# Where an attention loop issues its fills and weight loads: ahead of a turn's values, or behind them

## The reference

```python
x = x + jnp.tanh(g_xattn[0]) * _L0_xattn_ref(_layernorm(x), ctx_2048, ctx_2048)
x = x + jnp.tanh(g_ffn[0])   * _L0_ffn_ref(_layernorm(x), w_gate, wi_0, wi_1, wo)   # 8 experts, 2 per token
x = x + jnp.tanh(g_xattn[1]) * _L1_xattn_ref(_layernorm(x), ctx_2048, ...)          # scan over the context
x = x + jnp.tanh(g_ffn[1])   * _L1_ffn_ref(_layernorm(x), ...)                      # 64 experts, 4 per token
```

```python
qh = q.reshape(bs * 8, ch, T); kh = k.reshape(bs * 8, ch, S); vh = v.reshape(bs * 8, ch, S)
attn = softmax(einsum('bct,bcs->bts', qh * scale, kh * scale), axis=-1)
out  = einsum('bts,bcs->bct', attn, vh)
```

## Time and profile before

| what | value |
|---|---|
| time, median of 3 runs | 1125.35 us (1125.19 to 1127.35) |
| profiled execution | 1120.38 us, its span 1118.6 us |
| mean granted TensorE clock | 0.966 |
| TensorE busy | 1029.7 us, 92% |
| VectorE, ScalarE, GpSimd busy | 724.5, 500.5, 589.1 us |
| moved by DMA | 199.49 MB, mean 178 GB/s |

### The profile page before, as it was taken

How to read it: one execution, slowest core, us unless ns; L and a number is a source line. 1 busy time by engine, 2 the same in 40 slices (tenths; PEclk the granted TensorE clock), 3 DMA queues, 4 the chain that set the end, 5 groups by cost and what they waited for, 6 DMA issues and landing times. The chain is left out here.

```text
span 1118.6 us, 18847 instructions
## 1 busy us (share of the span) xinstructions
PE 1029.7 (92%) x5364; PEld 740.6 (66%) x5364; DVE 724.5 (65%) x1703; ACT 500.5 (45%) x880; POOL 589.1 (53%) x556
## 2 busy tenths in 40 slices
PE   5799999999878999999799999999999999999960
PEld 3455656655326777777279568578788888888850
DVE  4477777777547888887488438348415666666750
ACT  3375575564327888887342031221313333333320
POOL 6367767666324666667543646356342344434551
PEclk9899999999979999999899999999999999999985
DMA  9965556763543333332540231033269999999729
GB/s 285 348 211 186 165 186 222 246 221 119 198 146 126 124 103 106 105 108 85 186 159 1 107 113 56 25 128 106 89 221 324 337 325 309 287 312 341 194 27 194
DMA packets 128254, 199.49 MB, mean 178 GB/s; under 512 B 35975, under 2 KB 44167, under 8 KB 128186
## 3 DMA queue, kind: packets, MB, share of 16 engines
q1 hardware_dynamic: 106538, 160.66, 42.9%
q0 software_dynamic: 21360, 37.48, 13.3%
q10 hardware_dynamic: 288, 0.52, 0.1%
HBM read 133.10 MB, written 87.56 MB: 197 GB/s over the span
## 5 line engine op out<-in xcount | busy, mean ns | idle before, releaser
L935 POOL TENSOR_TENSOR m_down_lo<-wo,m_down_hi 128x512 fp32r<-128x512 f32 x78 | 129.4, 1679 | 75.9 <-ACT m_down_hi L1030 75.9
L543 PE MATMUL bank<-win,vT 128*128 128x512 f32 x256 | 124.4, 600 | 0.0
L703 DVE TENSOR_REDUCE negmax<-bank 128x1 bf16<-128x512 f32 x128 | 85.8, 674 | 46.0 <-PE bank L550 45.5
L633 ACT ACTIVATE win<-bank 128x512 f32<-128x512 f32 x128 | 69.4, 594 | 89.9 <-PE bank L535 89.4
L1044 DVE TENSOR_TENSOR m_up_lo<-w,m_up_hi 128x1024 fp32r<-128x1024 f32 x78 | 97.7, 1254 | 13.4 <-ACT m_up_hi L1002 11.9
L2035 POOL DMA_INDIRECT out<-m_y,m_token x32 | 50.7, 1586 | 85.3 <-DMA out<-m_y,m_token 34.1
L1264 POOL DMA_INDIRECT tab<-stage_up,slot x64 | 66.0, 1031 | 51.2 <-DVE slot L1610 33.3
L2065 PE MATMUL bank<-y,m_w 128*128 128x128 f32 x736 | 89.7, 275 | 0.0
L2035 POOL DMA_INDIRECT sums<-m_y,m_token x32 | 52.1, 1629 | 70.9 <-DVE m_y L2129 40.0
L2065 PEld LDWEIGHTS bank<-y,m_w 128*128 128x128 f32 x736 | 86.4, 193 | 0.1
L2179 ACT ACTIVATE sh_gate_a<-bank 128x512 f32<-128x512 f32 (+1 forms) x40 | 20.5, 512 | 146.9 <-PE bank L2172 146.9
(11 more groups left out here) (297 smaller groups left out, 2535.4 us busy)
## 6 DMA issues: line engine op xcount, KB each, us to landing
tab<-zeros SPq DMA_DIRECT2D x16, 1056.0 KB
m_w<-in_L_ffn_Wg SPq DMA_DIRECT2D x46, 256.0 KB, 4.5
m_w<-in_L_ffn_Wu SPq DMA_DIRECT2D x46, 256.0 KB, 4.9
m_w<-in_L_ffn_Wd SPq DMA_DIRECT2D x46, 256.0 KB, 6.1
m_x<-tab SPq DMA_DIRECT2D x39, 256.0 KB, 2.7
ytab<-m_y SPq DMA_DIRECT2D x39, 256.0 KB, 2.1
stage_up<-tab SPq DMA_DIRECT2D x32, 264.0 KB, 5.7
m_x<-tab SPq DMA_DIRECT2D x32, 264.0 KB, 5.9
```

The costliest lines, as they stand in the source:

```text
L543: nc.tensor.matmul(pO[s * 2 + h][:], vT[:, s, sb_, h:h + 2, :].rearrange("p a c -> p (a c)"), probs[:, sb_ % 2, h, :], start=(sb_ == 0), s ...
L633: nc.scalar.activation(probs[:, b % 2, h, :], pS[h][:], ACT.Exp, scale=1.0 / HEAD).then_inc(p_ready, 1)
L703: nc.vector.tensor_reduce(negmax[:, s, m:m + 1], rough_bank(k, m)[:], AX.X, ALU.max, negate=True).then_inc(pm_read, 1)
L935: nc.gpsimd.tensor_tensor(dn_lo[:, m, :], row(wo0, e * MB + m), dn_hi[:, m, :], ALU.subtract).then_inc(dn_lo_ready, 1)
```

## The change

The order of SyncE's program changes, and nothing else. The zero fill of the dummy rows and portion 0 move from ahead of the loop to behind it, portion 0 first. In each loop turn, portion u moves from between the even tile's keys and its values to behind these values; the odd tile's keys and values follow it, as before. The wait for `consts_ready` stays ahead of the loop. The number of DMAs, their sizes and their semaphores are the same.

```diff
             for t in range(2):
                 load_v(sp, t, t)
-            sp.wait_ge(consts_ready, 1)
-            sp.dma_start(T["tab0"][DUMMY_ROW:, :].rearrange("(r p) d -> p r d", p=P),
-                         zeros[:, 0:D].unsqueeze(1).broadcast_to([P, E0, D])).then_inc(s_zero1, 16)
...
-            behind(0)
+            sp.wait_ge(consts_ready, 1)
             with sp.Fori(1, TILES // 2) as u:
                 for n in range(2):
 
                     t = u * 2 + n
                     sp.wait_ge(k_lo_ready, t - 1)
                     load_k(sp, t, n)
+                    sp.wait_ge(p_used, u * 16 + (n * 8 - 8))
+                    load_v(sp, t, n)
                     if n == 0:
                         behind(u)
-                    sp.wait_ge(p_used, u * 16 + (n * 8 - 8))
-                    load_v(sp, t, n)
+            behind(0)
+            sp.dma_start(T["tab0"][DUMMY_ROW:, :].rearrange("(r p) d -> p r d", p=P),
+                         zeros[:, 0:D].unsqueeze(1).broadcast_to([P, E0, D])).then_inc(s_zero1, 16)
```

## The result

| what | before | changed |
|---|---|---|
| median | 1125.27 us (1123.39 to 1127.35, 4 runs) | 1147.55 us (1142.87 to 1155.86, 4 runs) |
| profiled execution | 1120.38 us, span 1118.6 | 1142.87 us, span 1141.1 |
| mean granted clock | 0.966 | 0.970 |

The account below looks back on a forecast made before the run. Attention was taken as bound by TensorE once running and by DMA at the opening. Terms -9.1 (opening), +29.4 (late odd keys), +7.2 (clock) and +1 (stage end) sum to +28.5 us on the median: 1154 us, range 1125 to 1168.

Parts of the forecast that it names:

- The opening, -9.1: Start of attention: tile 2's keys land before they are wanted, so the stall and its low clock go, -9.1 us.
- Odd keys 5.8 us late: Loop turns: the odd tile's keys queue behind the portion, so ScalarE's `k_hi` waits 5.8 us for them.
- A slip of 4.2 us per turn: Loop turns 1 to 7: late `k_hi` costs TensorE 4.2 us each, bounds 0 to 4.6, in all +29.4 us.
- nothing waits for them: Turns 2 to 7: the even tile's keys and values gain little, as nothing waits for them.
- the longest way: Late `k_hi` reaches TensorE through VectorE's reciprocal, 4.6 us late, the longest of three ways; 4.2 us was taken.
- this shape: Turns 1 to 7 were all taken to follow turn 2's pattern of late odd keys, 4.2 us each.
- rival 5: Both sides about even, with keys 2 to 3 us late: 1123 to 1128 us, chance 0.08.
- rival 4: Odd keys come in time as the portion drains at 400 GB/s; only the opening's 9.1 us remain: 1116, chance 0.15.
- The clock, +7.2: Loop: TensorE's idle gaps drop the granted clock in 3 of 7 turns at 2.4 us each, +7.2, bounds 0 and 16.8.
- rival 2: Late odd keys and the clock down in every turn: +38 us, 1163 us, chance 0.12.
- The end of the stage, +1: Portion 0 and the 2 MB fill behind the loop are just hidden; later context costs +1 us, bounds 0 and 5.
- The profiled execution and the median: The predicted +28.5 us was put on the runs' median of 1125.35 us, not on the profiled execution's 1120.38.

Follow-up runs that it names:

- The opening alone: Changed kernel with each loop portion back between the even tile's keys and values; fill and portion 0 stay behind the loop: 1117.28 us, ratio 0.9922.
- the fill of the sums: Changed kernel with the 0.52 MB fill of sums1 put back between the even tile's keys and values: 1138.0 us, ratio 1.0126.
- the loop without the drain: Changed kernel with zero fills moved behind the odd tile's values, weights left behind the even values, and GpSimd's drain replaced by a semaphore: 1125.68 us, ratio 1.0005.
- the two kernels with the drain: Changed kernel with weights back between even keys and values, 1135.1 us; changed kernel with zero fills moved behind the odd tile's values, 1148.72 us.
- the kernel without the drain: Changed kernel with GpSimd's drain ahead of the addition into x replaced by a semaphore, nothing else: 1155.41 us, ratio 1.0276.
- the split kernel: Changed kernel with the three weight blocks left behind the even tile's values and the three zero fills moved behind the odd tile's values: 1148.72 us, ratio 1.0199.

## Why the prediction was right

The forecast was 1154 us, and 1147.5 was measured, inside the forecast's own 1144 to 1160. Point by point:

**The opening, -9.1.** Right in mechanism, a little too large in size. The opening alone measured 9.1 us less than before, but with 6 to 11.5 by its interval and with the new end of the stage in it, so that the same figure came out is luck. In its trace `k_hi` of tiles 3 to 15 starts 7.9 us earlier than in the first profile of before, and 7.2 to 7.6 earlier than in the second.

**Odd keys 5.8 us late.** Right: 5.8 to 6.8 in the first profiled execution and 5.8 to 7.6 in the second, in each of seven turns, always for an odd tile. The order of issue is the order of landing, and the bytes between set it, as the fill of the sums showed.

**A slip of 4.2 us per turn.** Right in size, 3.7 to 4.2 in turns 2 to 6, but not by the way that was worked out, and so partly luck. The step "nothing waits for them" in turns 2 to 7 was incomplete. I counted the scattered rows as bytes and not as a wait: the portion is moved past GpSimd's DMAs too, and a drain on GpSimd waits for those. Half of the slip now comes there, before the odd keys are wanted. The sum came out right because the later wait covers this one. What the late keys cost by themselves is seen without the drain: a gap of 2.7 to 4.1 us in turns 2 to 6, all before the rough product that reads `k_hi`, and a low clock in each turn. That the 4.2 would come down the longest way, over the reciprocal, no run shows. Turn 1 does not have "this shape": it lost 5.4 and 6.9 us against the opening alone, with a gap of 3.7 and 4.8 us in one piece.

With keys about 2 us late, just below where rival 5 put "about even", the loop without the drain loses next to nothing. That this kernel measured 1125.7, within rival 5's bounds, is the context's wait at the end of the stage. The slack that rival 4 counts on is there. But the two kernels with the drain, and with keys as late, measured 1135 and 1149. So rival 5 as I priced it, and the point from which rival 4 decides, left the drain out.

**The clock, +7.2.** This term was mis-sized, and it is most of the difference. The changed kernel takes 30.3 us more than the opening alone (1147.55 and 1117.28), where the prediction had 29.4 + 7.2 = 36.6. The count was near, 2 and 4 turns in the two profiles against 3. The price of 2.4 us, taken from the opening, was not: there the clock was low from 43 to 50 us, here for 3.4 us. Turn 3 of the first profile, with a fall at the keys' wait, slipped by 5.5 us in place of 4; but in the second profile turns 5 and 6, with a fall ahead of the keys, slipped by 4.0 and 3.9. So a fall cost about 1.5 us, or nothing where the wait for the keys covered it. With two falls of the first kind in one profile and one in the other, I estimate the term at 1.5 to 3 us in place of 7.2.

Of rival 2 the Trainium skill (TensorE: Matmul & The Clock Gate, "HAM oscillation — how this bites in real kernels") tells of a loop in which every pass starts cold behind its DMA wait. In the changed kernel the trace does not agree: the clock fell at the wait for the keys in 2 and 1 of 7 turns. In the kernel without the drain it does, 7 of 7, and there the idle time stood in one piece.

**The end of the stage, +1.** Near, against one of the two profiles of before. The late context holds TensorE up less than before (3.53 us):

```profile
322.75 1.88 PE L496 MATMUL bank<-ctx_late,wsel 128*4 128x512 f32 x4 [1.11 <-DMA ctx_late<-in_ctx]
```

From the last values to the first mixture matmul it takes 38.7 and 39.1 us in the two profiles of the changed kernel. In the first profile of before it takes 42.2, with the low clock behind the gap of the earlier trace rows, and in the second 37.9, without it. So the end gave back 3.5 us against the first and cost 0.8 to 1.2 against the second.

**The profiled execution and the median.** Adding the 5 us between them came out right: the executions of before vary by more than that (1119.59 to 1130.57 us among 17), and the two profiles show two places of it, 7 us in a later stage and 5 us at this one's end, neither of which has to do with the change. Which of them made the first profile shorter than the median isn't settled, since they go opposite ways there.

## What to carry to other kernels

When a bulk transfer is moved in a queue, look at what is issued *behind* it: the small load that comes next is late by the bytes between, less its slack, in every turn. Then look at the other queue: scattered rows land later beside a full queue, and a drain on the engine that issued them can turn that into a wait which no trace row names (it stands as "issue"). Two such waits in one turn do not add; price each with the other taken away. And before a difference is put down to the loop, compare where the loop ends in the two traces: here a loss that looked like late keys stood behind it.

## What the hardware did that I had not expected

- A drain on GpSimd behind two indirect DMAs cost 1.6 us a tile (1148.72 to 1125.68 us by replacing it with a semaphore), though the two instructions around it don't touch the scattered data. It held GpSimd until the rows had landed: the addition behind it started 0.2 us after the landing, in the changed and the split kernel, in every tile whose landing the trace gives.
- The indirect DMAs took 5.3 us to land in turn 2 before and 7.0 after, with the whole portion queued beside them. The Trainium skill (DMA: Bandwidth & Descriptors, "Queues, rings and completion order") has the DMA engines take turns between queues packet by packet. By that a scatter would not have to stand behind the other queue's backlog. The trace of the changed kernel does not show it get ahead: the scatter issued at 77.03 us landed at 84.2, and so did the weight block issued at 76.47 on SyncE's queue, the last piece that was ahead of it there.
- The granted clock fell to 0.50 in some of the turns 1 to 7, for 3.4 or, without the drain, also 6.8 us. The short fall cost 1.1 to 1.9 us where nothing covered it, and nothing where it came while a wait for keys was still ahead; the long one cost about 1 us more.
